# Fewer stores per batch, clearing by slabs, and a later output product in a linear attention core

## The reference, cut to what matters

```python
x = L0_attn_x                                          # 16 batches, 256 tokens, 128 channels
x = x + 0.5 * ffn(layernorm(x), ...)
x = x + attn(layernorm(x), Wq, Wk, Wv, Wo)
x = x + 0.5 * ffn(layernorm(x), ...)

def attn(x, Wq, Wk, Wv, Wo):                           # linear attention, 16 heads of 8
    q, k, v = elu(x @ Wq.T) + 1, elu(x @ Wk.T) + 1, x @ Wv.T     # by heads
    kv_cumsum = cumsum(einsum('blhd,blhe->blhde', k, v), axis=1)
    k_cumsum = cumsum(k, axis=1)
    out = einsum('blhd,blhde->blhe', q, kv_cumsum)
    denom = clip(einsum('blhd,blhd->blh', q, k_cumsum), 1e-06, None)
    return (out / denom[..., None]) @ Wo.T

def ffn(x, ...):                                       # a transformer block
    h = layernorm(x, ln1)
    x = x + causal_softmax_attention(h)                # 16 heads of 8
    h = layernorm(x, ln2)
    return x + moe(h)                                  # 8 experts of 256 hidden, the top 2 per token
```

## Time and profile before

| | us |
|---|---|
| median of 3 executions | 1403.02 (1400.39 to 1404.61) |
| the profiled execution, its time | 1400.57 |
| its span, first to last instruction | 1398.8 |
| PE / DVE / ACT / POOL busy in it | 1026.4 / 1078.8 / 768.5 / 549.5 |
| first soft front and core | to about 432 |
| linear front, linear core | 576 to 688, 688 to 846 |
| last soft front | 846 to 911 |

### The profile page before, as it was taken

The page is one execution under the profiler, slowest core; times in us unless marked ns, Lnnn a source line. Parts: engine busy times, 40 slices in busy tenths (PEclk is TensorE's granted clock), DMA queues, the critical chain, the costliest instruction groups (busy, mean ns, idle before and its releaser), DMA issues.

```text
span 1398.8 us, 33588 instructions
## 1 busy us (share of the span) xinstructions
PE 1026.4 (73%) x11495; PEld 763.0 (55%) x11644; DVE 1078.8 (77%) x2383; ACT 768.5 (55%) x1170; POOL 549.5 (39%) x787
## 2 busy tenths in 40 slices
PE   2659688888862999466688876598888888559980
PEld 1537466666641666344355554466666666436660
DVE  5539599999985888588577776589999999558875
ACT  1228577777761555233455542288787778425550
POOL 2300245555564566311023321003555555636661
PEclk9869899999985999768888887899999999669995
DMA  3779411111001232234212102501111101023326
GB/s 95 218 219 358 132 36 40 43 46 46 29 20 42 84 87 83 83 91 128 74 56 62 51 27 76 151 18 37 48 46 42 44 29 32 18 62 87 91 68 190
DMA packets 147684, 111.58 MB, mean 80 GB/s; under 512 B 16240, under 2 KB 134512, under 8 KB 147568
## 3 DMA queue, kind: packets, MB, share of 16 engines
q1 hardware_dynamic: 129264, 87.09, 21.6%
q0 software_dynamic: 9088, 18.76, 4.0%
q10 hardware_dynamic: 9216, 4.20, 1.1%
HBM read 43.49 MB, written 59.82 MB: 74 GB/s over the span
## 4 chain that ended last, share of the span: by engine, by line
DVE 33%; issue 19%; PE 14%; ACT 10%; SPq 9%; POOL 8%; DMA 4%; DVEq 1%; ACTq 1%; POOLq 0%
DVE negm L1022 6%; SPq L1519 5%; POOL ys L1425 4%; DVE negm L1026 3%; DVE p_lo L1265 3%; ACT pf L839 2%; SPq L1498 2%; DVE x_all L980 2%; DVE pf L1272 2%; PE banks L422 2%; DVE p_lo L1034 2%; PE banks L457 2%; ACT p_hi L713 2%; DVE p_lo L1038 2%; DMA qk_d<-p_hi 2%
## 5 line engine op out<-in xcount | busy, mean ns | idle before, releaser
L696 ACT ACTIVATE pf<-banks 128x1536 f32<-128x1536 f32 x128 | 185.7, 1451 | 118.7 <-PE banks L444 93.1
L1034 DVE TENSOR_TENSOR p_lo<-pf,p_hi 128x1536 f16<-128x1536 f32 x128 | 223.8, 1749 | 7.8 <-ACT p_hi L713 6.8
L1402 POOL TENSOR_SCALAR rs<-mv 128x2 f32<-128x2 f32 x32 | 43.9, 1371 | 390.3 <-DVE mv L1087 307.2
L1425 POOL DMA_INDIRECT ys<-y_out,dest x156 | 151.2, 969 | 116.0 <-ACT y_out L845 91.0
L713 ACT CAST p_hi<-pf 128x1536 f16<-128x1536 f32 x128 | 188.7, 1474 | 2.0
L1376 POOL DMA_INDIRECT xs<-n_all,slot x128 | 167.1, 1306 | 54.6 <-issue 37.6
L1022 DVE TENSOR_REDUCE negm<-banks 128x4 f16<-128x1024 f32 x128 | 155.9, 1218 | 33.3 <-PE banks L422 24.1
L422 PE MATMUL banks<-kst,qst 96*128 96x128 f16 x1536 | 133.1, 224 | 48.1 <-DVE negm L1022 18.9
L444 PEld LDWEIGHTS banks<-ident,negm 128*128 128x128 f16 x1536 | 122.6, 100 | 83.3 <-issue 11.1
L437 PE MATMUL banks<-qst,kst 96*128 96x512 f16 x384 | 152.4, 397 | 7.9 <-ACT pf L696 7.9
L444 PE MATMUL banks<-ident,negm 128*128 128x128 f16 x1536 | 153.5, 224 | 0.3 <-issue 0.2
(11 more groups left out here) (197 smaller groups left out, 2486.8 us busy)
## 6 DMA issues: line engine op xcount, KB each, us to landing
xs<-zeros SPq DMA_DIRECT2D x20, 975.0 KB, 11.7
x_nats<-xs SPq DMA_DIRECT2D x78, 130.0 KB
qst<-qk_d SPq DMA_DIRECT2D x192, 48.0 KB
kst<-qk_d SPq DMA_DIRECT2D x48, 192.0 KB
qk_d<-p_hi SPq DMA_DIRECT2D x128, 64.0 KB, 2.1
pf<-ys SPq DMA_DIRECT2D x32, 256.0 KB, 3.2
v_hl<-v_all SPq DMA_DIRECT2D x48, 136.0 KB
qk_d<-p_lo SPq DMA_DIRECT2D x96, 64.0 KB, 2.1
```

Source lines behind the costliest of these rows:

```text
L696: nc.scalar.activation(pf[:, g % 2, :, :, :].rearrange(flat), banks_t[:, :, :].rearrange("p a b -> p (a b)"), ACT.Exp, scale=HD ** -0.5).t ...
L1034: nc.vector.tensor_tensor(lo, pf[:, g % 2, :, :, :].rearrange(flat), hi, ALU.subtract)\
L1425: nc.gpsimd.indirect_dma_start(ys, bass.IndirectOffsetOnAxis(ap=dest[:, t % YB, h:h + 1], axis=0), y_out[:, t % YB, h, :], None).then_inc( ...
```

## The change

**Stores.** `qk_d` is laid out with the 128 channels outermost and six slots in each: k low, q high, k high, q high, k high, q low. ACT writes slots 1 to 4 in one transfer of 256 KB from the high halves, read twice, in all three phases; SP writes the two low halves. The loads take every second slot. **Clearing.** 16 slabs: slab n is rows n * 256 to n * 256 + 255 of each expert's 4096, eight transfers of 130 KB; before it SP waits until the slabs before have landed. Slabs 0 to 2 go out behind the expert weights, slab b behind the load of batch b, and one transfer for the remaining 5,888 rows at the end. The scatter of batch b waits for slabs 0 to b. **Linear core.** The turn of b-1 stands behind values 1 of b, the Wo product of b-1 behind values 3 of b, one batch later; DVE's back_add stands before the context; ACT copies the turned context after reading values 0 and 1, and that reading waits for the context of b-1. The soft core's order stays.

```diff
-STORES = 16 * 6
+STORES = 16 * 3
-ZN = -(-ROWS // (ZR * P))
+ZU = 2
+SLABS = CAP // TS
+SLAB = 16 * E
-        qk_d = nc.dram_tensor("qk_d", [B, 2, G * GH, 3, HD, T * P], F16).ap()
+        qk_d = nc.dram_tensor("qk_d", [B, P, 6, T * P], F16).ap()
PE, iteration:
-                    if g == 3 and place > 0:
+                    if ph["soft"] and g == 3 and place > 0:
                         back_turn(ph, b - 1)
...
-                    if g == 3 and place > 0:
+                    if ph["soft"] and g == 3 and place > 0:
                         back_wo(ph, b - 1)
+                    if not ph["soft"] and g == 1 and place > 1:
+                        back_wo(ph, b - 2)
+                    if not ph["soft"] and g == 3 and place > 0:
+                        back_turn(ph, b - 1)
PE, after the last batch:
+                else:
+                    back_wo(ph, B - 2)
ACT, store_high (now called in all phases):
-                for k in range(2):
-                    nc.scalar.dma_start(qk_d[b, k, :, 0, :, :], qk_hi[:, b % RB, k, :])\
-                        .then_inc(ph["stored"][b % RB], 16)
+                nc.scalar.dma_start(qk_d[b, :, 1:5, :].rearrange("p (a k) m -> p a (k m)", a=2),
+                                    qk_hi[:, b % RB, :, :].rearrange("p k m -> p (k m)").unsqueeze(1)
+                                    .to_broadcast([P, 2, 2 * T * P])).then_inc(ph["stored"][b % RB], 16)
ACT, pv_read:
+                if not ph["soft"] and hf == 0 and not (isinstance(b, int) and b == 0):
+                    sc.wait_ge(ph["cx_in"], ph["n"] * B + b)
ACT, iteration:
-                    if g == 3 and place > 0:
+                    if ph["soft"] and g == 3 and place > 0:
                         ctx_turned(ph, b - 1)
...
                     if g == 3:
                         pv_read(ph, b, 0)
+                    if not ph["soft"] and g == 3 and place > 0:
+                        ctx_turned(ph, b - 1)
DVE, iteration:
-                    if g == 0 and place > 1:
+                    if g == (0 if ph["soft"] else 2) and place > 1:
                         back_add(ph, b - 2)
POOL, scatter:
-                    if ph is phases[0] and b == 0:
-                        gp.wait_ge(blank, 16 * ZN)
+                    if ph is phases[0]:
+                        gp.wait_ge(blank, SLAB * (b + 1))
SP:
+            def clear_slab(n):
+                sy.wait_ge(blank, SLAB * n)
+                for e in range(E):
+                    row = e * CAP + n * TS
+                    sy.dma_start(xs[row:row + TS, :].rearrange("(p r) d -> p (r d)", p=P), zeros[:, :])\
                         .then_inc(blank, 16)
+            def clear_rest():
+                sy.wait_ge(blank, SLAB * SLABS)
+                rest = xs[E * CAP:ROWS, :].rearrange("(p a r) d -> p a (r d)", p=P, r=ZU)
+                sy.dma_start(rest, zeros[:, :].unsqueeze(1).to_broadcast([P, (ROWS - E * CAP) // (P * ZU), ZU * RW]))\
+                    .then_inc(blank, 16)
SP, store:
-                own = () if ph["soft"] else ((0, qk_hi),)
-                for k, parts in ((0, ((1, qk_hi), (2, qk_lo))), (1, ((1, qk_lo), (2, qk_hi)))):
-                    for r, src in own + parts:
-                        sy.dma_start(qk_d[b, k, :, r, :, :], src[:, ring, k, :]).then_inc(ph["stored"][ring], 16)
+                for k, slot_no in ((0, 5), (1, 0)):
+                    sy.dma_start(qk_d[b, :, slot_no, :], qk_lo[:, ring, k, :]).then_inc(ph["stored"][ring], 16)
SP, attention:
-                    if ph is phases[0] and b % 2:
-                        clear_rows([b // 2])
...
                 if ph is phases[0]:
                     load_experts()
-                    clear_rows(range(B // 2, ZN))
+                    for n in range(RB):
+                        clear_slab(n)
                 for b in range(RB, B):
                     load(ph, b)
+                    if ph is phases[0]:
+                        clear_slab(b)
+                if ph is phases[0]:
+                    clear_rest()
SP, experts:
+                sy.wait_ge(blank, SLAB * SLABS + 16)
```

## The result

The changed kernel takes 1328.88 us (median of 4 runs, 1324.23 to 1331.67) against 1401.70 for the kernel before (4 runs): ratio 0.9476, 95% interval 0.9439 to 0.9512. The forecast was 1348, its range 1328 to 1372. The profiled execution has a span of 1329.9 us, 68.9 less than before.

A forecast was written before the change was run, and what follows sets the result against it. Engines were taken to wait for SP's issues of stores and clears, not for work. Gains of 10.4, 21.9, 1.4, 12.0 and 8 sum to 54 us, giving 1347 or 1349, stated as 1348, range 1328 to 1372.

The forecast's parts named there:

- Last front: Front of the last soft phase: fewer SP stores end it sooner and group 1 is turned earlier, 10.4 us won.
- the 2.13 us: Soft fronts: time of one step on VectorE where nothing waits, taken as the new step's length.
- The price of a store, 0.64: Fronts: each store assumed to hold its issuing engine 0.64 us, ScalarE's 256 KB one included.
- First front: Front of the first soft phase: ends at 71.1 instead of 90.4 and group 1 follows sooner, 21.9 us won.
- Batch 3: First core: its load no longer queues behind 13 big clears, so VectorE's 12.0 us stall goes.
- The queue's arithmetic: SP behind the first front: slabs 0 to 2 issued by 99.3, batch 3's load landing near 107, wanted near 121.
- Linear front: Linear phase's front: ACT's wait for SP's last store goes, less 0.5 us for its new issue, 1.4 us won.
- Linear core: Linear core's loop: new order cuts it from 9.55 to 9.0 us (8.2 at full clock), 8 us over 14 batches.
- (a): Rival, linear core: the wait only moves, group 0 also runs at the low clock, 5 us lost, 1361; chance 0.11.
- (b): Rival, soft fronts: held by data movement, not issue, so they keep their pace, 1376; chance 0.06.
- (c): Rival, clearing: a slab's clears go one after the other, 16.4 us per slab, batch 3's load 11 late, 1359; chance 0.06.
- (d): Rival, clearing: each small clear holds SP 2.67 us, so the kernel is slower, 1467; chance 0.04.

The follow-up runs named there:

- e1: The kernel before with only the change's three stores per batch, old clearing and linear core kept: 1360.2 us, ratio 0.9719.
- e4: The changed kernel with ScalarE's one 256 KB store issued as two of 128 KB: 1336.6 us, ratio 0.953.
- e5: The changed kernel with its new qk_d layout but the old six 64 KB stores per batch, from their old engines: 1338.1 us, ratio 0.956.
- e2: The kernel before with only the change's clearing by slabs: 1374.4 us, ratio 0.9815.
- e7: The changed kernel with each small clear issued as two of half the size, 16 per slab: 1332.7 us, ratio 0.9521.
- e9: The changed kernel with the linear core's turn of the context put back ahead of group 3's products: 1360.3 us, ratio 0.9704.
- e11: The changed kernel with VectorE's context ahead of the sum in the linear core, and second and third early loads after batches 13 and 15: 1325.7 us, ratio 0.9456.
- e8: The changed kernel measured again without any edit, as the measure for later runs on its chip: 1328.4 us, ratio 0.9486.
- e6: The changed kernel with VectorE working the previous batch's context ahead of the sum (back_add) in the linear core: 1326.1 us, ratio 0.945.
- e12: The changed kernel with VectorE's context ahead of the sum in the linear core, and all three early loads after batches 13, 14 and 15: 1327.6 us, ratio 0.9485.
- e10: The changed kernel with the second and third early load of each front issued after batches 13 and 15, not 9 and 12: 1327.2 us, ratio 0.9469.

## Why the prediction was right, and where its terms were off

The direction and every place of the gain were right, and 1328.88 is at the lower end of the range. Four of five terms were too small: 71.7 us came from the places where 52.3 were expected, and three of them lie above their own upper bounds. That the time is still inside the range is in part luck: with the linear front the stages gave 72.4 us, more than the 70 of all upper bounds together, which from the median of 1403.0 end at 1333; the range happened to reach 5 us further.

**Last front: 10.4 forecast, 18.1 measured, above the upper bound of 13.5.** The mechanism, SP's issues holding the ring of stored buffers, is what e1 shows. The step that failed is the 2.13 us, mis-sized as what a front's step takes where nothing waits. In those steps ScalarE was full, with two stores of 0.59 each (rows of the kernel before under e4). With one store, even at the prediction's own 0.64, ScalarE needs 1.6 us (2.13 - 1.18 + 0.64, an estimate), so the new step is VectorE's own 1.89, as e1 and the changed kernel have it: 11 x 0.24 = 2.6 us. The price of a store, 0.64, was too high as well: the 256 KB one issues in 0.37, a 64 KB one of SP in the new layout in 0.46, and the layout, whose reading was put at nothing, made even a load cheaper on SP (in the last front 2.5 us in e5, 2.9 before). So SP catches up sooner: the early loads cost 1.4 us where 3 were allowed, and the last two steps are shorter. Behind the front's end (831.04 + 0.69) group 1 is turned 8.5 us later, not 10.25: that figure came from the first front of the kernel before, and I took it for the work itself. TensorE's first product of group 1 in both cores, which answers to the earlier trace rows:

```profile
77.26 0.38 PE L437 MATMUL banks<-qst,kst 96*128 96x512 f16 x1 [0.34 <-ACT pf L701]
...
840.23 0.38 PE L437 MATMUL banks<-qst,kst 96*128 96x512 f16 x1 [0.61 <-ACT pf L701]
```

**First front: 21.9 forecast, 27.1 measured** (26.0 at the turn of group 1, 103.30 to 77.26), above the bound of 25, for the same step of 2.13. The prediction put it down to stores and clears together without splitting it; e1 and e2 do: 17.8 and 12.0.

**Batch 3: 12.0 forecast, 13.5 measured, above the bound of 12.** VectorE's waits for TensorE's scores in the kernel before, between 126 and 176 us, show why:

```profile
DVE negm L1022 <- PE banks L422: 13.5, 2, 12.0
```

The 12.00 was the longer of two waits of the same batch. The queue's arithmetic held otherwise, though its terms end at 104 and not at the 107 it gives; e7 shows at least 10 us of room. And of the window from 103 to 154 VectorE stood 10.8 us for batch 3, not 12, since the wait ends at 155.20; that the traffic costs the core next to nothing is borne out by its 49.2 of 51 us after the change.

**Linear front: 1.4 forecast, 0.7 measured**, between the expert stage's first sum (579.2 and 540.0) and the core's first relu (688.3 and 648.4).

**Linear core: 8 forecast, 13.0 measured.** The loop was right as far as e9 shows: without the turn's new place nothing is won. Its fast end, 8.2, is there in the intervals at the full clock. The slow ones average 9.15, near its slow end of 9.05, and reach 9.5: in that interval group 1's products stand 0.43 apart (from 705.60 to 706.03), as forecast, and the values between them are slow too. I had taken the slow end for all 14. With the mix 11.5 came, and 1.5 more from the last interval (6.91 to 5.42), which the sum had left out.

**The rivals.** (a) has one thing right: TensorE stands 1.4 us per batch before the turn after the change as before (12.6 us in 9 waits, and 12.3 in 9). It is the work queued behind the wait that changed. (b) is refuted by e1 and e5: same bytes, 19.9 and 9.5 us sooner. The Trainium skill (DMA: Bandwidth & Descriptors, Issuing engines are not separate DMA queues) calls the sequencer's time usually small beside the transfer; here it was the bound, four issues of 0.64 us in a step that needs 1.89, and the trace does not agree. The Trainium skill (Perfetto Trace Analysis, What "DMA-bound" means) does name an issuing engine full of such slices as a bound of its own, and the rows of SP agree, with a store every 0.64 us. (c) and (d) are refuted by SP's 24 clears in 19.67 us, and by e7's 48 in 30.91.

No version was shown to beat the changed kernel: e11 has the lowest median of the four on its chip, 1325.7 against 1328.4 for e8, and overlapping intervals.

## What to carry to other kernels

Price a transfer on the issuing engine by the row of its own shape, and look at the layout as well as the count: the even stride took about as much from the last front (8.6 us) as halving the number of stores did after it (7.1). Ask of every step that is read off one engine which engine set it: the 2.13 us stood on VectorE's timeline, but were ScalarE's. Where a waiting instruction can't be made to wait less, move what is queued behind it ahead of it; the other edits of the same loop may be worth nothing, or worse, without that. Where a loop has a price at two clocks, carry both into the sum, since the intervals may alternate.

## What the runs showed of the hardware

The time that an engine is held by one store did not rise with its bytes. On ScalarE it was 0.59 us for 64 KB into 16 blocks, 0.41 for 64 KB at an even stride (e5), 0.42 for 128 KB (e4) and 0.37 for 256 KB; on SP 0.63 and 0.46 for the first two. Which property of the pattern sets it was not separated further. And the order of VectorE's work moved the clock granted to TensorE: e6, e11 and e12 had four or five of 15 linear intervals over 8.5 us, at granted clocks of 0.73 to 0.82 in e6, the changed kernel, e7, e8 and e10, whose linear core is the same but for that order, seven to nine. The matmuls are the same in all.
